# A decoder block on one core: the first two layer normalisations applied by ScalarE instead of VectorE

## What is computed

```
x = layernorm(x + attn(x))        # rotary memory trace: cumsum(v * rotor) * conj(rotor), times Wo
x = layernorm(x + xattn(x, ctx))  # decayed scores, divided by max(|row sum|, 1), times ctx
x = layernorm(x + ffn(x))         # router, top 2 of 8 experts, SwiGLU experts

def layernorm(x, eps=1e-5):
    m = mean(x); v = var(x)       # over the 256 features of a token
    return (x - m) / sqrt(v + eps)
```

## Time and profile before

| | before |
|---|---|
| time, median of 3 runs | 270.92 us (lowest 270.89) |
| span of the profiled execution | 269.3 us |
| TensorE busy | 208.4 us, 77% |
| VectorE busy | 169.8 us, 63% |
| ScalarE busy | 116.8 us, 43% |
| GpSimd busy | 153.1 us, 57% |
| mean granted TensorE clock | 0.915 |

### The profile page before, as it was taken

The page is one execution under the profiler, slowest core; times in us unless marked ns, Lnnn a source line. Parts: engine busy times, 40 slices in busy tenths (PEclk is TensorE's granted clock), DMA queues, the critical chain, the costliest instruction groups (busy, mean ns, idle before and its releaser), DMA issues.

```text
span 269.3 us, 5242 instructions
## 1 busy us (share of the span) xinstructions
PE 208.4 (77%) x1393; PEld 184.8 (69%) x1394; DVE 169.8 (63%) x534; ACT 116.8 (43%) x286; POOL 153.1 (57%) x140
## 2 busy tenths in 40 slices
PE   8387698988989998857899999999999999400000
PEld 8387587977978888757688888888888888300000
DVE  5945988889889768595355455455554554207993
ACT  4352251433424420381345545454554554515665
POOL 1264857747756720085567777777777774515330
PEclk9889999999999999995999999999999999855555
DMA  7945456656543100550223223233332332079413
GB/s 222 392 163 179 136 194 223 168 176 198 205 164 119 39 22 21 189 166 2 88 79 104 86 94 99 86 97 100 97 96 87 97 95 78 12 213 318 171 78 156
DMA packets 20130, 35.75 MB, mean 133 GB/s; under 512 B 2861, under 2 KB 11312, under 8 KB 20112
## 3 DMA queue, kind: packets, MB, share of 16 engines
q1 hardware_dynamic: 16368, 26.21, 29.6%
q0 software_dynamic: 3744, 9.31, 11.3%
HBM read 27.12 MB, written 9.31 MB: 135 GB/s over the span
## 4 chain that ended last, share of the span: by engine, by line
PE 62%; DVE 17%; issue 9%; POOL 4%; DMA 4%; ACT 2%; DVEq 1%; SPq 0%; ACTq 0%; POOLq 0%
PE p_c L558 13%; PE p_v L558 7%; PE p_y L480 6%; PE p_y L584 4%; PE p_r L558 4%; PE p_a L558 4%; PE p_s L464 3%; PE p_s L558 3%; PE p_v L420 3%; PE p_t L597 3%; POOL space L1020 3%; DVE space L851 3%; PE p_r L508 2%; PE p_a L499 2%; PE p_t L446 2%
## 5 line engine op out<-in xcount | busy, mean ns | idle before, releaser
L558 PE MATMUL p_c<-w_hi,parts 128*128 x104 | 34.6, 414 | 0.0
L1044 POOL DMA_INDIRECT y_dram<-x1T,scatter_now x26 | 26.3, 1013 | 11.8 <-issue 5.3
L1024 POOL DMA_INDIRECT turns<-x_dram,gather_now x26 | 25.4, 979 | 12.6 <-issue 3.8
L823 DVE TENSOR_TENSOR parts<-p_y,parts 128x256 fp32r<-128x256 f32 x39 | 16.5, 424 | 17.6 <-ACT parts L934 17.6
L1011 POOL TENSOR_TENSOR w_lo<-keep,w_hi 128x1536 fp32r<-128x1536 f32 (+1 forms) x8 | 27.5, 3434 | 0.1
L833 DVE TENSOR_TENSOR cs<-p_c,cs 128x256 f32<-128x256 f32 x26 | 11.0, 425 | 22.6 <-ACT cs L941 22.6
L994 POOL TENSOR_TENSOR space<-back 128x512 f32<-128x512 f32 x8 | 10.2, 1271 | 18.9 <-DVE back L717 18.9
L941 ACT ACTIVATE cs<-p_c 128x256 f32<-128x256 f32 x26 | 10.1, 387 | 24.6 <-PE p_c L558 24.6
L437 PE MATMUL p_c<-const,space 128*128 128x128 f32 x128 | 17.3, 292 | 4.2 <-DVE space L671 4.2
L664 DVE TENSOR_SCALAR x<-r,mv,rs 128x256 f32<-128x256 f32 x32 | 20.2, 671 | 0.6
L1002 POOL TENSOR_TENSOR cs<-space,vinv 128x256 f32<-128x256 f32 x16 | 9.5, 612 | 18.5 <-DVE vinv L731 15.0
(11 more groups left out here) (161 smaller groups left out, 575.0 us busy)
## 6 DMA issues: line engine op xcount, KB each, us to landing
keep<-in_weights SPq DMA_DIRECT2D x8, 768.0 KB, 4.4
space<-y_dram SPq DMA_DIRECT2D x16, 256.0 KB, 4.2
space<-in_xT SPq DMA_DIRECT2D x8, 256.0 KB, 3.5
keep<-in_x SPq DMA_DIRECT2D x8, 256.0 KB, 3.5
space<-in_ctxT SPq DMA_DIRECT2D x8, 256.0 KB, 2.8
space<-in_ctxt SPq DMA_DIRECT2D x8, 256.0 KB, 3.1
x_dram<-x SPq DMA_DIRECT2D x8, 256.0 KB, 2.2
keep<-x_dram SPq DMA_DIRECT2D x1, 2048.0 KB, 8.4
```

Source lines behind the costliest of these rows:

```text
L558: last = nc.tensor.matmul(dst, lhs[:, k, :], w[:].rearrange("p e n -> p (e n)")[:, bass.ds(start + col + k * width, width)], start=(n == 0 ...
L823: nc.vector.tensor_tensor(xs_lo[s], p_xt, xs_hi[s].bitcast(F32), ALU.subtract).then_inc(xlo_ok, 1)
L1024: nc.gpsimd.indirect_dma_start(xs[s], None, x2_dram, bass.IndirectOffsetOnAxis(ap=gather_now[s][:], axis=0)).then_inc(xs_ok[s], 16)
L1044: nc.gpsimd.indirect_dma_start(y_dram, bass.IndirectOffsetOnAxis(ap=scatter_now[s][:], axis=0), ys[s], None, bounds_check=TOPK * N - 1, oo ...
```

## The change

Both normalisations of the first stage are applied by ScalarE. VectorE keeps the reciprocal and adds one `scalar_tensor_tensor` of 128x2, move = -mean * rs, for each (buffers `move1` and `move2`, semaphores `shift1_ok` and `shift2_ok`). ScalarE computes x1 (and x2) as src * rs + move with two ACTIVATEs of 128x256, x1 between sd1 and x1T, x2 between sd2 and vabs. Two waits are new on VectorE: the next r2 waits for x2_ok, and the next r1 for x1_ok, since ScalarE now reads r2 and r1.

```
-            def normalise(j, src, mv, sd, rs, dst, sd_ok, rs_ok, dst_ok):
+            def scales(j, mv, sd, rs, move, sd_ok, rs_ok, move_ok):
                 dve.wait_ge(sd_ok, j + 1)
                 nc.vector.reciprocal(rs[:], sd[:]).then_inc(rs_ok, 1)
                 dve.wait_ge(rs_ok, j + 1)
-                for q in range(2):
-                    last = nc.vector.tensor_scalar(dst[:, q, :], src[:, q, :], mv[:, q, 0:1], rs[:, q:q + 1],
-                                                   ALU.subtract, ALU.mult)
-                last.then_inc(dst_ok, 1)
+                nc.vector.scalar_tensor_tensor(move[:], mv[:, :, 0], -1.0, rs[:], ALU.mult, ALU.mult).then_inc(move_ok, 1)
...
                 if has(-2):
                     dve.wait_ge(av_ok, i - 1)
+                    if has(-3):
+                        dve.wait_ge(x2_ok, i - 2)
                     nc.vector.tensor_tensor(r2[:], p_a[:], x1[s][:], ALU.add).then_inc(r2_ok, 1)
                 if has(-1):
-                    normalise(i - 1, r1, mv1, sd1, rs1, x1[1 - s], sd1_ok, rs1_ok, x1_ok)
+                    scales(i - 1, mv1, sd1, rs1, shift1, sd1_ok, rs1_ok, shift1_ok)
...
                 if has(-2):
-                    dve.wait_ge(x2_free, i - 1)
-                    normalise(i - 2, r2, mv2, sd2, rs2, x2[s], sd2_ok, rs2_ok, x2_ok)
+                    scales(i - 2, mv2, sd2, rs2, shift2, sd2_ok, rs2_ok, shift2_ok)
...
                 if has(0):
                     dve.wait_ge(y_ok, i + 1)
                     dve.wait_ge(x_ok[s], 8 * (i - s) + 16)
+                    if has(-1):
+                        dve.wait_ge(x1_ok, i)
                     nc.vector.tensor_tensor(r1[:], p_y[:], x_in[s], ALU.add).then_inc(r1_ok, 1)
...
+            def normalise(src, rs, move, dst, dst_ok):
+                for q in range(2):
+                    last = nc.scalar.activation(dst[:, q, :], src[:, q, :], ACT.Identity,
+                                                scale=rs[:, q:q + 1], bias=move[:, q:q + 1])
+                last.then_inc(dst_ok, 1)
+
             def step(i, s, has):
                 if has(-1):
                     act.wait_ge(mv1_ok, 2 * i)
                     nc.scalar.activation(sd1[:], mv1[:, :, 1], ACT.Sqrt, bias=eps[:]).then_inc(sd1_ok, 1)
+                    act.wait_ge(shift1_ok, i)
+                    normalise(r1, rs1, shift1, x1[1 - s], x1_ok)
                     act.wait_ge(t1_ok, i)
                     nc.scalar.activation(x1T[:], p_t[:], ACT.Copy).then_inc(x1T_ok, 1)
                 if has(-2):
                     act.wait_ge(mv2_ok, 2 * i - 2)
                     nc.scalar.activation(sd2[:], mv2[:, :, 1], ACT.Sqrt, bias=eps[:]).then_inc(sd2_ok, 1)
+                    act.wait_ge(shift2_ok, i - 1)
+                    act.wait_ge(x2_free, i - 1)
+                    normalise(r2, rs2, shift2, x2[s], x2_ok)
                 if has(-1):
                     act.wait_ge(sum_ok, i)
                     nc.scalar.activation(vabs[:], rowsum, ACT.Abs).then_inc(vabs_ok, 1)
```

More of the change, by code:

```diff
@@ L168, in decoder_block @@
         shift = [sb(f"shift{s}", [P, 2]) for s in range(2)]
+        shift1, shift2 = sb("move1", [P, 2]), sb("move2", [P, 2])
         st_pair, mv_pair, sd_pair, rs_pair = [st1, st2], [mv1, mv2], [sd1, sd2], [rs1, rs2]
@@ L292, in decoder_block @@
         x2_free = sem("x2_free")
+        shift1_ok, shift2_ok = sem("shift1_ok"), sem("shift2_ok")
         x2_out = [sem(f"x2_out{s}") for s in range(2)]
```

## The result

The changed kernel takes 284.3 us (median of 5 runs, 283.63 to 287.41), against 270.92 us before. The comparison of the runs gives 1.0525 times as long, with a 95% interval of 1.0477 to 1.0573 (the quotient of the two medians is 1.049). It leaves out one execution of the kernel before that took 373.49 us; the four others lie between 270.36 and 271.82. The direction and the place were predicted, the size was not: 280.5 us had been forecast, with a range to 284.0. The profiled execution of the changed kernel is the longest of the five (287.41 us, span 285.5 us), so sums are taken from the differences inside the first stage, and not from the spans.

The account below looks back on a forecast made before the run. The prediction took the first stage's loop through GpSimd's w_lo, 10.85 us a step, as the bound. Its terms, 5.2 + 3.9 + 0.5 = 9.6 us over 270.92, gave 280.5 us, with a range of 276.5 to 284.

Parts of the forecast that it names:

- What bounds the kernel: First stage: a closed loop from T1 through GpSimd's cs, xT_lo and w_lo to x1, period 10.85 us.
- First term: At x1: move1 held until w_lo's end, then ScalarE's pair; T1 +0.65 us in each of eight steps, +5.2 us.
- Second term: x2 on ScalarE before vabs delays vabs, then cs to w_lo: +0.56 us in each of seven steps, +3.9 us.
- Third term and routing: Stage's end: last x2 takes 1.25 us instead of 0.74, +0.5 us; VectorE's routing, queued behind vabs, +0.56 us.
- The whole: Whole kernel: +9.6 us, span 278.9 us and time 280.5 us, 3.6% slower.
- TensorE's clock falls: Rival: longer idle before T1 drops TensorE to 1.2 GHz, some 1.8 us in each of seven steps, up to 293 us; chance 0.04.
- move1 is not held: Rival: move1 beside w_lo takes 0.14 us, T1 then follows from the reciprocal; about 270.5 us; chance 0.08.
- What costs nothing: First stage: x2's later readiness, later w_hi, VectorE's waits on x1_ok and x2_ok, and L499's 0.5 us longer wait add nothing.

Follow-up runs that it names:

- 5 and 1 filled: Changed kernel plus unread matmuls in TensorE's idle time, 5 before the wait for x1, 1 before that for cs; 279.32 us, 1.031 times before.
- The kernel with the mean in PSUM: Changed kernel with mean and variance of r1 in PSUM, so move1 has one SBUF input instead of two; 270.68 us, 0.9945 times before.
- second profile: The changed kernel run once more, unaltered, as partner of the filled runs on the same chip; 284.04 us, 1.0485 times before.

## Why the prediction was wrong, point by point

- **What bounds the kernel**: right. The loop through GpSimd was the bound: the kernels that take w_lo off it and leave x2 on VectorE are faster, by 1.7% and twice 2.5%.
- **First term, +0.65 us a step**: right. T1 stood 1.19 to 1.20 us behind w_lo's end in almost every step (1.18 predicted), and 4.7 us over seven steps were measured against 4.6.
- **Second term, +0.56 us a step**: right. 3.5 us over six steps against 3.4; both terms together 8.2 us against 7.9.
- **Third term and routing**, 0.56 + 0.5 = 1.06 us from the last T1 to the last transposes of x2: right. It was 107.60 - 95.80 = 11.80 us; now it is 124.66 - 111.80 = 12.86.

```profile
124.66 0.66 PE L493 MATMUL p_t<-const,x 128*128 128x128 f32 x4 [1.29 <-ACT x L893]
```

- **The whole**: with the clock kept (5 and 1 filled), the profiled span is 277.9 us, 8.6 over before, where 9.6 was forecast. It is 0.1 us ahead of the first T1 (0.65 forecast), 8.2 in the seven steps (7.9), 1.05 to the last transposes of x2 (1.06), and 0.7 less behind these (161.0 against 161.7 us, forecast unchanged). What is missing lies outside the stage's loop.
- **"TensorE's clock falls", chance 0.04**: this is the step that failed. The sum of 9.6 us has no term for the clock, and the range only "one or two microseconds" (284 against 282.7). I had taken one row, the 2.17 us wait with a clock of 1.00, as proof that a wait of 1.9 us is safe. In the full steps the waits came out as computed (1.85 to 1.97 us); the wait that had been 2.17 grew too, to 2.85. The clock fell in five of the seven steps in the first profile and in three in the second, each time for some 3.4 us. Beside the same step of the filled kernel, such a step is 0.9 to 1.4 us longer, which makes 5.7 and 3.5 us; the prediction had 1.8 us a step, and all seven steps or none. With the clock kept by filling, the changed kernel is 4.7 us shorter (284.04 and 279.32 us) and ends within 1.2 us of the 280.5 predicted. None of the signs that the prediction named for its being wrong came up, since none was about the clock.
- **"move1 is not held", 0.08**: the duration that was to decide it is 0.8 to 1.9 us beside w_lo, so the rival fell. Its time was worked out at about 270.5 us, 0.4 less than before. The kernel with the mean in PSUM, which makes it true, took 270.68, but where before took 272.60: it is 0.9945 times before, some 1.5 us less, and had a step at 0.84. So the two figures stand close together by luck in part.
- **What costs nothing**: right as far as it was seen. No row among VectorE's waits of the first stage is ended by ScalarE's x1 or x2, so the new waits on x1_ok and x2_ok cost nothing that can be seen. L499 did wait longer for cs (0.4 us), and the filled steps match the sum without a cost of it.

Open: why the clock falls in one step and not in another that looks alike. The length of the wait alone does not decide it. In the second profile of the changed kernel a wait of 1.95 us stands before a step with 1.00 and another before a step with 0.87, and the longest, 2.84 us, before a step with 1.00; with x1 alone on ScalarE, a wait of 1.84 us stands before a step with 0.87.

## What to carry to other kernels

Before moving work away from an engine, ask what the instruction waits for. Here x1 was not slow but held by a GpSimd instruction beside it, and what replaced it, though 256 times smaller, had two inputs in SBUF and was held until the same moment, with a hop to another engine behind it. Keeping r1, from which x1 is made, in PSUM took the hold away without moving any work to another engine, and gave 2.5% where the move cost 5%. And where TensorE's wait on a loop grows, price the clock too, as a share of the steps and not as all or nothing.

## What the runs showed of the hardware that was not expected

TensorE's granted clock fell to 0.50 for some 3.4 us in some of the steps that begin with a wait of 1.84 us or more, though in before it had stayed at 1.00 after one of 2.17, and in the changed kernel's second profile after one of 2.84. The matmuls in that stretch run at 1.2 GHz: transposes take up to 1.11 us for 0.66, scores up to 2.07 for 1.13, and the step becomes 0.9 to 1.4 us longer. A scalar_tensor_tensor of 128x2 with two inputs in SBUF took 0.16 us alone and up to 1.94 beside w_lo, ending with it; with one of them in PSUM, 0.16 beside w_lo too. A tensor_scalar of 128x256 that reads PSUM took 0.54 us, beside GpSimd or not; the one that reads SBUF took 0.41 us alone and up to 2.17 beside w_lo.

The scores at the low level, from the second profile of the changed kernel:

```profile
61.09 1.97 PE L466 MATMUL p_s<-x1T,space 128*128 128x128 f32 x8 [0.17 <-issue]
```
